# Opening loads reordered: first adjacency pair in two transfers, row loads released as pairs land, bias addition behind the 31st adjacency transfer

## What is computed

```python
# layer 0: only the last 100 neighbours of a row count, halved with each step back
rank = jnp.cumsum(mask, axis=1)
deg = rank[:, -1:]
k = jnp.minimum(deg, float(MAX_NEIGH))
pos = rank - (deg - k)
w = mask * jnp.where(pos > 0, DECAY ** (k - pos), 0.0)
out = w @ support + bias
# layer 1: two gated steps (GRU form) on adj @ (x @ W)
# layer 2: (dinv * (adj + I) * dinv) @ x @ W
# layer 3: concat(x, (adj @ x) / deg) @ W.T
x = _layernorm(x + _L0_gnn_ref(x, adj, L0_gnn_weight, L0_gnn_bias), axis=-1)
```

## Time and profile before

| what | value |
|---|---|
| three runs | 503.36, 503.38, 503.71 us, median 503.38 |
| profiled execution, first to last instruction | 501.7 us |
| the profiled execution's own whole time | not listed apart; the median is 1.7 us above its span |
| TensorE (PE) busy | 474.5 us (95%) |
| ScalarE (ACT) busy | 223.9 us (45%) |
| VectorE (DVE) busy | 189.5 us (38%) |
| GpSimd (POOL) busy | 113.3 us (23%) |
| mean granted TensorE clock | 0.985 |
| longest DMA queue, q0 (issued by POOL) | 9216 packets, 16.78 MB, 33.4% of 16 engines |

### The profile page before, as it was taken

The page is one execution under the profiler, slowest core; times in us unless marked ns, Lnnn a source line. Parts: engine busy times, 40 slices in busy tenths (PEclk is TensorE's granted clock), DMA queues, the critical chain, the costliest instruction groups (busy, mean ns, idle before and its releaser), DMA issues.

```text
span 501.7 us, 6728 instructions
## 1 busy us (share of the span) xinstructions
PE 474.5 (95%) x2546; PEld 220.5 (44%) x2546; DVE 189.5 (38%) x697; ACT 223.9 (45%) x391; POOL 113.3 (23%) x154
## 2 busy tenths in 40 slices
PE   4939999999999999999999999999999999999993
PEld 1303333343334433545445444444446555555572
DVE  3230030015005500644543528666645443255354
ACT  2836878879887788143322333333211011021110
POOL 3075222106200300141211112432333323211111
PEclk9977999999999999999999999999999999999997
DMA  8949999999999900000000000000000000000000
GB/s 120 134 57 106 107 108 106 108 107 108 107 107 107 106 1 1 0 1 0 2 0 2 1 0 2 0 1 0 2 0 1 0 2 0 2 12 22 22 12 21
DMA packets 13899, 20.02 MB, mean 40 GB/s; under 512 B 2856, under 2 KB 5676, under 8 KB 13868
## 3 DMA queue, kind: packets, MB, share of 16 engines
q0 software_dynamic: 9216, 16.78, 33.4%
q1 hardware_dynamic: 4364, 2.63, 2.0%
q10 hardware_dynamic: 288, 0.20, 0.2%
HBM read 68.88 MB, written 1.05 MB: 139 GB/s over the span
## 4 chain that ended last, share of the span: by engine, by line
PE 83%; DVE 5%; DMA 4%; SPq 2%; POOL 2%; issue 2%; ACT 1%; POOLq 0%
PE Y L753 38%; PE both L710 11%; PE Y L684 10%; PE both L712 10%; DMA w_y<-in_w 3%; PE both L666 3%; PE both L664 3%; PE both L669 2%; PE both L660 1%; PE both L672 1%; PE both L674 1%; DMA adjT<-in_adjT 1%; PE turn L618 1%; POOL xrow L248 1%; SPq L188 1%
## 5 line engine op out<-in xcount | busy, mean ns | idle before, releaser
L753 PE MATMUL Y<-adjT,S 128*128 128x512 fp8e4 (+1 forms) x1056 | 230.1, 373 | 1.0 <-POOL S L235 0.9
L318 ACT ACTIVATE wgt<-both 128x512 int16<-128x512 f32 x256 | 152.7, 597 | 41.6 <-PE both L712 24.8
L753 PEld LDWEIGHTS Y<-adjT,S 128*128 128x128 f16 x1056 | 101.9, 99 | 107.8 <-POOL S L235 1.4
L710 PE MATMUL both<-adjT,fix 128*128 128x512 fp8e4 x248 | 95.1, 383 | 9.3 <-DMA adjT<-in_adjT 9.3
L712 PE MATMUL both<-adjT,tri 128*128 128x512 fp8e4 x256 | 98.6, 385 | 0.0
L684 PE MATMUL Y<-wgt,S 128*128 128x512 bf16 x256 | 97.8, 382 | 0.0
L220 POOL TENSOR_TENSOR rstd<-stat,mhalf 128x4 f32<-128x4 f32 (+2 forms) x29 | 31.2, 1076 | 222.2 <-DVE stat L405 222.2
L710 PEld LDWEIGHTS both<-adjT,fix 128*128 128x128 bf16 x248 | 24.0, 97 | 87.6 <-ACT wgt L318 53.8
L448 DVE TENSOR_TENSOR rz<-both,consts 128x512 f32<-128x512 f32 x4 | 2.8, 692 | 131.1 <-PE both L733 131.1
L243 POOL DMA_DIRECT2D adjT<-in_adjT x64 | 34.9, 577 | 45.6 <-DMA adjT<-in_adjT 44.8
L684 PEld LDWEIGHTS Y<-wgt,S 128*128 128x128 f16 x256 | 25.2, 99 | 30.1 <-issue 1.4
(11 more groups left out here) (100 smaller groups left out, 365.5 us busy)
## 6 DMA issues: line engine op xcount, KB each, us to landing
adjT<-in_adjT POOLq DMA_DIRECT2D x64, 256.0 KB, 31.5
xrow<-in_xrow SPq DMA_DIRECT2D x8, 128.0 KB, 11.2
out_rows<-xrow SPq DMA_DIRECT2D x7, 128.0 KB, 1.9
consts<-in_consts ACTq DMA_DIRECT2D x1, 128.0 KB, 4.9
out_rows<-xrow SPq DMA_DIRECT2D x2, 64.0 KB, 1.6
consts<-in_consts ACTq DMA_DIRECT2D x1, 64.0 KB, 3.1
w_y<-in_L3WT SPq DMA_DIRECT2D x4, 16.0 KB, 18.3
m<-in_whh1T SPq DMA_DIRECT2D x2, 32.0 KB
```

The costliest lines, as they stand in the source:

```text
L318: nc.scalar.activation(wgt[:, c, t % 2, :], V[c][:, :], ACT.Relu).then_inc(w_ready[c], 1)
L710: nc.tensor.matmul(V[c][:, :], fix[:, :], adj_tile(q, jb + 1, c), start=False, stop=False, skip_group_check=True)
L753: mm = nc.tensor.matmul(Y[g % 2][:, 0:nb * P], S[layer % 2][:, jb, :], cols[:, jb, :], start=(jb == 0), stop=(jb == JB - 1), skip_group_ch ...
```

## The change

1. The first pair goes out as two transfers, one tile each, with a semaphore of its own for the first; TensorE starts its first step when that tile has landed.
2. Of the eight row loads only the first is issued at once. Block G-2-n is issued after pair n has landed, so SP waits in turn for pairs 0 to 6. The bias and the loads of `w_y` are issued between these waits, and the gate weights behind the last.
3. POOL no longer waits after pair 6. The bias addition, with its three waits, stands behind transfer i = 30.

```diff
--- before.py
+++ after.py
@@ -125,6 +125,7 @@
 
 
         load = [sem(f"load{i}") for i in range(NLOAD)]
+        first_tile = sem("first_tile")
         small_in = sem("small_in")
         gate_zero = sem("gate_zero")
         gate_in = sem("gate_in")
@@ -183,16 +184,26 @@
 
         @block.sync
         def _(sp):
-            for g in range(G - 1, -1, -1):
+            def load_x(g):
+
                 blk = slice(g * B, (g + 1) * B)
+                if g < G - 1:
+                    sp.wait_ge(load[G - 2 - g], 16)
                 sp.dma_start(xrow[:, blk, :], a["xrow"][:, blk, :]).then_inc(x_in[g], 16)
+
+            load_x(G - 1)
+            load_x(G - 2)
+            load_x(G - 3)
             sp.dma_start(bias0[:, :], a["bias"].to_broadcast([P, D])).then_inc(small_in, 16)
             for half in range(2):
                 rows = slice(half * D, (half + 1) * D)
                 sp.dma_start(w_y[rows, 0:D], a["L2W"]).then_inc(small_in, 16)
                 sp.dma_start(w_y[rows, D:2 * D], a["L3WT"][D:2 * D, :]).then_inc(small_in, 16)
+                load_x(G - 4 - half)
                 sp.dma_start(w_y[rows, 2 * D:3 * D], a["L3WT"][0:D, :]).then_inc(small_in, 16)
                 sp.dma_start(w_y[rows, 3 * D:4 * D], a["w0"]).then_inc(small_in, 16)
+            for g in range(G - 6, -1, -1):
+                load_x(g)
             for l in range(2):
                 for half in range(2):
                     rows = slice(half * D, (half + 1) * D)
@@ -240,8 +251,13 @@
                     if i >= NLOAD:
                         pool.wait_ge(load[i % NLOAD], 16 * (i // NLOAD))
                     jp = JP - 1 - n
-                    pool.dma_start(adjT[:, q, 2 * jp:2 * jp + 2, :], a["adjT"][q, jp]).then_inc(load[i % NLOAD], 16)
-                    if i == 6:
+                    if i == 0:
+                        for half, landed in ((1, first_tile), (0, load[0])):
+                            pool.dma_start(adjT[:, q, 2 * jp + half, :], a["adjT"][q, jp][:, 2 * GC * half:2 * GC * (half + 1)])\
+                                .then_inc(landed, 16)
+                    else:
+                        pool.dma_start(adjT[:, q, 2 * jp:2 * jp + 2, :], a["adjT"][q, jp]).then_inc(load[i % NLOAD], 16)
+                    if i == 2 * NLOAD - 2:
                         pool.wait_ge(const_ready, CONSTS)
                         pool.wait_ge(small_in, SMALL)
                         pool.wait_ge(s_ready, G)
@@ -694,7 +710,11 @@
             for q in range(Q):
                 for t in range(JB):
                     jb = JB - 1 - t
-                    if t % 2 == 0:
+                    if q == 0 and t == 0:
+                        pe.wait_ge(first_tile, 16)
+                    elif q == 0 and t == 1:
+                        pe.wait_ge(load[0], 16)
+                    elif t % 2 == 0:
                         i = q * JP + t // 2
                         pe.wait_ge(load[i % NLOAD], 16 * (i // NLOAD + 1))
                     for c in range(2):
```

## The result

| | before | changed kernel |
|---|---|---|
| median | 503.54 us (503.36 to 504.02) | 513.47 us (513.10 to 513.93) |
| ratio to before | | 1.0192, 95% interval 1.0178 to 1.0207 |
| span of the profiled execution | 501.7 us | 511.5 us |
| mean granted TensorE clock | 0.985 | 0.972 |

The changed kernel is slower by 9.9 us. Forecast were +7.5 us and 510.9 us, with a range of 501 to 516.

A forecast was written before the change was run, and what follows sets the result against it. TensorE, busy 95% of 501.7 us, was taken as the bound. Gate products starting at 69.5 instead of 64.37 (+5.1) grew to +7.2 by quarter 1's first step; 0.3 more made +7.5 us: 510.9 us, range 501 to 516.

The forecast's parts named there:

- The one-to-one exchange: DMA queues: while POOL's queue has work, SP's gets one packet per POOL packet, however small; gate_in full at 69.5 us.
- Small loads overtake: Rival, SP's queue: several small packets pass per POOL packet, no wait for gate_in, 12.2 us faster, 491; chance 0.14.
- in part: Rival, SP's queue: small loads overtake partially, gate_in full between 58 and 64, time 499 to 505; chance 0.07.
- Turns by transfer: Rival, DMA queues: switching only once per transfer, 98.5 us in place of 59.0, kernel at 550; chance 0.02.
- row loads released by pairs: Opening, SP's queue: empty until pair 0 lands at 8.3, then 1.4 us to first packets; restarts at 9.7 (8.0 to 11.5).
- the release does nothing for pair 0: Rival, opening: pair 0 in at 9.8, SP's queue starts 1.5 us later, 512.4 us; no chance of its own.
- The drain: SP's queue after its restart: row loads 20.2, small loads 35.3, bias rows 3.5, together 59.0 us, plus 0.8 for landing.
- the bias rows' 3.5 us: End of SP's queue: 12 packets of bias rows on one of 16 engines cost 3.5 us, 0.2 if they spread.
- Behind the wait: After gate_in: DVE conversions and half-clock products put PE at 74.35 instead of 67.13, plus 0.3 for later half clock.
- What was to be hidden: Quarter 0: PE's wait of some 3 us at step 17 and its 2 us gain vanish in the 14.5 us gate_in wait.
- The bias addition: POOL, behind transfer 30: runs to about 51 while DVE waits for gate_in, costs nothing; uncovered, up to 4.44 us.

The follow-up runs named there:

- only_pool: Kernel before with only POOL's bias addition moved from behind transfer 6 to behind transfer 30: 503.13 us, ratio 0.9995.
- no_release: Changed kernel without SP's waits for pairs ahead of the row loads: 500.48 us, ratio 0.9944 to the kernel before.
- packed: Changed kernel with w_y in one transfer, gate weights in three, bias rows in one: 493.79 us, ratio 0.9810 to the kernel before.
- bias_rows_packed: Changed kernel with the six loads of bias rows made one load of two rows: 511.01 us, ratio 1.0150 to the kernel before.
- pe_kept_busy: Changed kernel with 50 unused matmuls on PE between quarter 0 and its wait for gate_in: 513.13 us, ratio 1.0183 to the kernel before.
- packed_no_release: Changed kernel with w_y, gate weights and bias rows in fewer transfers and without SP's waits for pairs: 493.04 us, ratio 0.9796.
- packed_all_at_once: Kernel before with w_y, gate weights and bias rows in fewer transfers and the bias addition behind transfer 30: 493.42 us, ratio 0.9799.

## Why the prediction was right

**The one-to-one exchange** was right, and it decided everything: 448 to 448 and 111 to 108 in the trace before, 2105 to 2107 in the trace after. Three kernels (only_pool, no_release, packed) differ in when SP's queue may start and in how many packets it has, and `gate_in` moved to 61.30, 59.01 and 46.76 us, where 61 to 62 was expected for the first two and 46 for the third; no_release came 2 us early by the half-size packets. One number of the argument is wrong: `w_y` has 8 x 80 = 640 packets, not some 300. The sums use 22 x 80 and do not change.

**Small loads overtake**, in full or in part: did not happen. The 362 packets against 45 were, as argued, those of a microsecond in which POOL's queue ran out. **Turns by transfer** did not happen either: loads of 80 packets took their turns packet by packet, 540 to 540 from 50 to 60 us; by transfers `gate_in` would have come at 9.7 + 98.5 + 0.8 = 109 us. The Trainium skill (DMA: Bandwidth & Descriptors, section "Queues, rings and completion order") has an engine drain a packet of some 9 to 17 descriptors before it switches; the counts of this trace do not show such turns. By my estimate from the counts, 80 packets are 5 an engine and 144 are 9, so whole shares in turn would have given 5 to 9.

**The size** was 2.4 us short, and the step that was mis-sized is "row loads released by pairs", the time at which SP's queue starts again. I had it at 9.7 us, and it was about 13.3. The timeline of SP, the DMA table from 12 to 13.5 us, and DVE at the block's landing:

```profile
9.85 2.89 SPq L192 DMA_DIRECT2D xrow<-in_xrow  x2
```

```profile
q0 software_dynamic: 88, 0.16, 106.1%
q1 hardware_dynamic: 8, 0.01, 2.0%
```

```profile
17.07 0.29 DVE L494 TENSOR_SCALAR S<-xrow 128x256 f16<-128x256 f32 x1 [11.75 <-DMA xrow<-in_xrow]
```

Two parts of it were off. Pair 0 as two transfers was whole at 9.85 and not at 8.3, no sooner than the 9.24 of the single transfer; my upper bound had been 9.8. That is the rival "the release does nothing for pair 0", and as to pair 0 it came true: from 5 to 10 us SP's queue passed no packet in the changed kernel, and in no_release, with all row loads out, PE could start step 1 at 9.13 without a wait for the second tile. And the load issued at 9.85 had moved 8 packets by 13.5: over 3 us from issue to first packets, where I allowed 1.4 and bounded with 2.9. The queue thus started about 13.3. That rival had 1.5 us for the late pair; the longer way from issue to first packets, about 2 us more than I allowed, came on top and has no cause that the runs show. The start was 3.6 us late; 1.1 us less in the drain and 0.2 behind the wait leave the 2.4 that the sum was short.

**The drain** I put at 59.0 us and 0.8; from 13.3 to 72.04 it took 58.7 with the tail, 1.1 us less, which hid a part of the late start. So the paces of 49.8 and 54 packets a us and the bias rows' 3.5 us (2.3 of them taken away by bias_rows_packed) held as a sum.

**Behind the wait** I put 2.4 us (2.1 to the second half of the step and 0.3 after); measured were 1.76 and 0.4. The mechanism of the first held: PE's second products at half pace, which DVE's second pick awaits. The conversions lie within that time, and pe_kept_busy shows that they alone would cost 0.89 of the 1.76. The 0.4 I had put down to the half clock; 0.33 of it is a wait for ScalarE's weights.

**What was to be hidden** was: PE waited 3.73 us at step 17 (3 expected) and arrived at `gate_in` at about 60.1 instead of 55. That is mainly the late start of SP's queue again: DVE had row block 3 at 38.02 where I had 33.6, and PE left step 17's wait only then. The late second tile, and the half pace of the matmuls after it (the one at 9.88 took 0.61 us), only made that wait shorter, since PE came to it at 35.1 instead of 31. All of it vanished in the wait, which shrank to 11.9 us from the 14.5 expected. The bias addition ran from 51.12 to 55.6 us, where I had 46 to 51, and cost PE nothing: with 15 pairs out, PE has no wait for a pair between 9.88 and 90 us.

## What to carry to other kernels

Beside a long queue of bulk transfers, a load from another queue cost, in these kernels, its number of packets times the time of a bulk packet, with hardly a difference between packets of 1 KB (49.8 a us) and small ones (54): pack small constants into few transfers with long rows, and count their packets against the time at which they are needed. A pause in the bulk queue that looks like waste may be what lets the small loads through; before taking it away, find out who comes last without it. Here the pause and the small packets had to go together: packed_no_release and packed_all_at_once beat both kernels by 10 us over the one before and by 20 over the changed one.

## What the runs showed of the hardware that I had not expected

- A load issued by SP into an idle queue of its own, while POOL's queue was full, moved its first packets over 3 us after its issue (issue at 9.85, 8 packets by 13.5). In packed, too, the load issued at 9.34 had its first packets after 12.5, and the block reached DVE at 16.41. I did not try what sets this delay.
- Packets of POOL's queue at half the size passed at 75 a us beside SP's, against 43 of full size, in the same microsecond of two kernels; a split transfer gives the other queue more turns, 146 by 10 us.
- Six one-row loads, 12 packets and some 3 KB in all, stretched the end of SP's queue: made into one load of 4 packets, `gate_in` was full 2.3 us earlier.
